# Three passes on high and low halves for the q, k, v projections of a fused attention and feed-forward kernel

## The chip, the core and the metric

The kernel runs on one core of a Trainium2 chip. Time is device time in microseconds (us) of one execution; the median of several runs counts. The core has a matrix engine (TensorE, in the profile PE, its weight loads PEld), a vector engine (VectorE, DVE), an activation engine (ScalarE, ACT), GpSimd (POOL) and a queue for transfers (SyncE, SP). Each engine works off its own list of instructions in order; the lists are tied together by semaphores.

## The reference

`x` has 64 batches of 32 rows by 512 numbers. With C = 32 rows per batch, the computation is, in float32 where nothing else is said:

```python
W = cond_w[condition]                        # one 32x32 matrix per batch
xm = einsum('bct,bcd->bdt', x, W)            # the mix
q, k, v = split(xm @ Wqkv + bqkv)            # 512 -> 3 x 128
a = softmax(q @ k.T / sqrt(128))             # 32 x 32 per batch
x2 = x + (a @ v) @ Wo + bo                   # 128 -> 512
g = sigmoid(conv5(mean of x2 over the first length[b] of 512 columns))
h = dequant(quantize_mx(x2 * g))             # fp8 e4m3, one power of two per 32 numbers
out = x2 + bfloat16(h @ dequant(quantize_mx(ffn_w)).T + ffn_b)
```

## The kernel before

The 2048 rows are 16 tiles of 128 rows (four batches each); two tiles are a unit, so there are 8 units u = 0 to 7, and t = 0 or 1 is the tile in its unit. The quantiser treats the two halves of the weight `ffn_w` as steps 0 and 1 and unit u as step u + 2.

For a unit TensorE does, in this order of dependence: `mix(u, t)` (ps_mix, eight float32 matmuls of 128 columns), `project_qk(u, 0)` for q, `project_qk(u, 1)` for k and `project_v(u)` (four float32 matmuls of 256 columns each, from `wqkv_f` and `xc`), `scores`, `attend` (probabilities times v), `project_out(u, t)` (with Wo), `convolve`, then two loop steps later `ffn(u, t)`. Between them ScalarE copies PSUM to SBUF: `copy_mix` writes `xc` from ps_mix, `copy_qk` q_t and k_t, `copy_v_t`, `copy_v`, `copy_o`, `copy_ffn`; it also makes the exponentials and, as `magnitude`, the absolute values for the rounding. VectorE does the softmax (`score_max` writes negmax; `softmax_inverse`, `softmax_divide`, then four `softmax_turn` write prob_t), the residual sums x2 out of ps_wo, `masked_sum`, `block_max`, the scales (scale, inv, inv_g), `scaled` (h), `round_sum` (h_sum), `round_back` (h_round) and `clip`. GpSimd does `residual` (xb = x + bo), `dequantise` (xq) and most of `final_sum` (result).

The order on each engine is written out by hand. The loop over s = 0 to 6 holds on TensorE: transposes of step s, `turn_v(s)`, `project_qk(s+1, 0)`, `attend(s)`, `mix(s+2, .)`, `project_out(s, 0)`, `project_qk(s+1, 1)`, `project_out(s, 1)`, `scores(s+1)`, `ffn(s-2, 0)`, `project_v(s+1)`, `convolve(s)`, `ffn(s-2, 1)`. `project_out(s, 1)` waits for VectorE's residual sum of tile 0, since both use the bank ps_wo. `convolve(s)` waits for `masked_sum(s, 1)`. GpSimd's `residual(s+1)` stands behind `final_sum(s-2, 1)`, which waits for `copy_ffn(s-2, 1)` on ScalarE and so for `ffn(s-2, 1)`. On ScalarE `copy_mix(s+2, 1)` stands behind `copy_qk(s+1)`, which waits for `project_qk(s+1, 1)`.

Ahead of the loop VectorE works on the weight halves (steps 0 and 1 of the quantiser) and the band matrix of the convolution while the first transfers land, and ScalarE issues four small transfers of `mix_w` itself: `gather_unit_1((2, 3))` stands behind `magnitude(0, 0)` and `magnitude(0, 1)`.

Of the kernel before, what the change touches and what calls it, by code (L numbers as in the profile page):

```python
# [52 lines left out]
def adaln_attn_ffn_kernel(  # L53
# [32 lines left out]
    with ExitStack() as ctx:  # L86
        def sb(name, shape, dt):
            return ctx.enter_context(nc.sbuf_tensor(name, shape, dt))
# [321 lines left out]
        def _(pe):  # L410
# [19 lines left out]
            def project_qk(u, which):  # L430

                if which == 0:
                    if u == 0:
# [8 lines left out]
                if which == 1:  # L442
                    mm.then_inc(qk_done, 1)

            def project_v(u):
# [3 lines left out]
                for c in range(TC):
                    mm = nc.tensor.matmul(ps_v[:], wqkv_f[:, c, 2 * D:3 * D], xc[:, u % 2, c, :],  # L450
                                          start=(c == 0), stop=(c == TC - 1))
                mm.then_inc(v_done, 1)
# [647 lines left out]
```

## Time and profile before

| | |
|---|---|
| time, median of 3 runs | 169.82 us (169.04 to 169.82) |
| time of the profiled execution | 170.97 us |
| its span, first to last instruction | 169.3 us |
| busy: PE, DVE, ACT, POOL | 130.5, 134.9, 65.4, 64.6 us |
| mean granted TensorE clock | 0.879 of full |

The profiled execution lies 1.15 us above the median, and 1.7 us of it are outside its span. "Busy" adds up the time in which an engine had an instruction under way; it doesn't say which engine the end waits for, which is read from the chain of waits and from the order of time.

### The profile page before, as it was taken

How to read it: one execution, taken by the hardware profiler on the slowest of the kernel's cores; microseconds unless marked ns; L12 is line 12 of the kernel's file. 1: busy time of each engine (PE TensorE's matmuls, PEld its weight loads, DVE VectorE, ACT ScalarE, POOL GpSimd, SP SyncE). 2: the span in 40 equal slices, each digit the busy share in tenths (PEclk: the TensorE clock that was granted, in tenths of full speed). 3: DMA queues.
4: the chain of work that ended last, by engine and by line, in shares of the span. 5: the costliest groups of instructions: out<-in, count | busy, mean ns of one | idle time of the engine just before them, and what ended most of it. 6: DMA issues, size and time to landing. Idle time of an engine off the chain costs nothing.

```text
span 169.3 us, 2698 instructions
## 1 busy us (share of the span) xinstructions
PE 130.5 (77%) x738; PEld 90.4 (53%) x738; DVE 134.9 (80%) x279; ACT 65.4 (39%) x158; POOL 64.6 (38%) x48
## 2 busy tenths in 40 slices
PE   6902899699679889959994999499929955947492
PEld 2402789586477676647573867376716633323130
DVE  4198299759987989899989797978799699599932
ACT  0110433554552646426451545144523463106321
POOL 5330058005612902580555055505551553254500
PEclk9985559999978999999999699959995996587959
DMA  4979103040400000042016001100110011101033
GB/s 112 330 216 321 41 15 122 4 129 6 129 8 2 0 0 0 12 148 98 4 64 187 9 3 64 62 0 0 66 62 0 0 62 62 46 18 41 25 124 124
DMA packets 9489, 11.49 MB, mean 68 GB/s; under 512 B 3954, under 2 KB 4466, under 8 KB 9474
## 3 DMA queue, kind: packets, MB, share of 16 engines
q1 hardware_dynamic: 7186, 8.62, 15.2%
q10 hardware_dynamic: 2096, 2.64, 4.9%
q0 software_dynamic: 192, 0.05, 0.5%
q8 instruction: 6, 0.10, 0.2%
q14 instruction: 9, 0.07, 0.2%
HBM read 7.12 MB, written 4.19 MB: 67 GB/s over the span
## 4 chain that ended last, share of the span: by engine, by line
PE 65%; issue 13%; DVE 6%; DMA 5%; POOL 3%; ACT 3%; SPq 2%; POOLq 1%; ACTq 0%; DVEq 0%
PE ps_qk L439 17%; PE ps_mix L426 12%; PE ps_wo L498 10%; PE ps_v L450 8%; PE ps_ffn L535 7%; DMA mix_w<-in_L_cond_weights_dram 5%; PE ps_att L481 3%; POOL xq L373 2%; PE ps_ffn L533 2%; PE ps_att L471 2%; DVE inv_g L929 1%; PE ps_v L460 1%; SPq L303 1%; PE ps_tr L517 1%; DVE mix_w L972 1%
## 5 line engine op out<-in xcount | busy, mean ns | idle before, releaser
L373 POOL TENSOR_TENSOR xq<-h_clip,scale 128x1024 bf16<-128x1024 bf16 (+1 forms) x11 | 23.1, 2104 | 55.8 <-DVE h_clip L967 37.3
L439 PE MATMUL ps_qk<-xc,wqkv_f 128*128 128x256 f32 x128 | 33.1, 407 | 0.8 <-ACT xc L648 0.8
L439 PEld LDWEIGHTS ps_qk<-xc,wqkv_f 128*128 128x128 f32 x128 | 26.3, 210 | 9.2 <-issue 5.9
L426 PE MATMUL ps_mix<-mix_w,x_sb 128*128 128x128 f32 x128 | 20.8, 331 | 7.5 <-DMA mix_w<-in_L_cond_weights_dram 7.5
L426 PEld LDWEIGHTS ps_mix<-mix_w,x_sb 128*128 128x128 f32 x128 | 19.7, 242 | 8.0 <-issue 7.9
L656 ACT ACTIVATE h_mag<-h 128x512 bf16<-128x512 f32 x20 | 12.4, 625 | 27.4 <-DVE h L941 27.4
L294 POOL TENSOR_TENSOR result<-ffn_out,x 128x512 f32<-128x512 bf16 x12 | 14.5, 1208 | 20.7 <-ACT ffn_out L715 20.7
L498 PE MATMUL ps_wo<-wo_f,o_t 128*128 128x512 f32 x30 | 19.0, 722 | 1.0 <-ACT o_t L663 1.0
L363 POOL TENSOR_TENSOR xb<-x_sb,bo_row 128x1024 f32<-128x1024 f32 x8 | 19.2, 2397 | 0.0
L950 DVE SCALAR_TENSOR_TENSOR h_sum<-h_mag,h 128x512 f32<-128x512 bf16 x20 | 13.7, 691 | 6.8 <-ACT h_mag L656 5.9
L481 PE MATMUL ps_att<-prob_t,v_sb 128*128 128x128 f32 x32 | 5.9, 311 | 15.9 <-issue 15.9
L535 PE MATMUL ps_ffn<-wq_t,xq_t 128*128 128x512 bf16 x56 | 17.0, 433 | 0.0
L450 PE MATMUL ps_v<-xc,wqkv_f 128*128 128x256 f32 x64 | 15.3, 383 | 0.0
L855 DVE TENSOR_TENSOR x<-ps_wo,xb 128x512 f32<-128x512 f32 x15 | 10.3, 688 | 5.4 <-PE ps_wo L498 5.3
L481 PEld LDWEIGHTS ps_att<-prob_t,v_sb 128*128 128x128 f32 x32 | 4.7, 207 | 18.4 <-issue 18.3
L648 ACT ACTIVATE xc<-ps_mix 128x512 f32<-128x512 f32 x16 | 9.6, 597 | 11.8 <-PE ps_mix L426 11.8
L958 DVE SCALAR_TENSOR_TENSOR h_round<-h_mag,h_sum 128x1024 bf16<-128x1024 bf16 (+1 forms) x11 | 12.4, 1128 | 1.0
L450 PEld LDWEIGHTS ps_v<-xc,wqkv_f 128*128 128x128 f32 x64 | 12.0, 190 | 2.1
L715 ACT ACTIVATE ffn_out<-ps_ffn 128x512 bf16<-128x512 f32 x14 | 8.3, 596 | 12.3 <-PE ps_ffn L535 12.3
L864 DVE SCALAR_TENSOR_TENSOR masked<-pos_f,len_f,x 128x512 f32<-128x512 f32 x16 | 12.9, 805 | 0.0
L671 ACT ACTIVATE q_t<-ps_qk,bq_scaled 128x256 f32<-128x256 f32 x8 | 3.8, 473 | 21.1 <-PE ps_qk L439 21.1
L941 DVE TENSOR_TENSOR h<-x,inv_g 128x512 f32<-128x512 f32 x16 | 11.3, 749 | 0.2
(86 smaller groups left out, 198.0 us busy)
## 6 DMA issues: line engine op xcount, KB each, us to landing
out_dram<-result SPq DMA_DIRECT2D x16, 256.0 KB, 2.0
x_sb<-in_x_dram SPq DMA_DIRECT2D x7, 512.0 KB
ffn_w_f<-in_L_ffn_weight_dram ACTq DMA_DIRECT2D x2, 512.0 KB, 8.6
mix_w<-in_L_cond_weights_dram SPq DMA_DIRECT2D x56, 4.0 KB, 1.6
wqkv_f<-in_L_attn_Wqkv_dram ACTq DMA_DIRECT2D x1, 768.0 KB, 5.4
x_sb<-in_x_dram SPq DMA_DIRECT2D x2, 256.0 KB, 6.4
bias_row<-in_L_ffn_bias_dram ACTq DMA_DIRECT2D x1, 256.0 KB, 5.6
bo_row<-in_L_attn_bo_dram ACTq DMA_DIRECT2D x1, 256.0 KB, 7.6
```

Source lines behind the costliest of these rows:

```text
L294: engine.tensor_tensor(result[:, t, :], ffn_out[:, t, :], x2[:, u % 3, t, :], ALU.add) \
L363: nc.gpsimd.tensor_tensor(xb[:, u % 2], x_sb[:, u], bo_row[:].to_broadcast([P, SUB, T]), ALU.add) \
L373: nc.gpsimd.tensor_tensor(xq[:, v % 2, t0:t1].rearrange("p t (n k) -> p (t n) k", k=BLOCK), h_clip[:, v % 2, t0:t1].rearrange("p t (n k) - ...
L426: mm = nc.tensor.matmul(ps_mix[t][:, c, :], x_sb[:, u, t, c * P:(c + 1) * P], mix_w[:, u, t, :], start=True, stop=True)
L439: mm = nc.tensor.matmul(ps_qk[:, which, :], wqkv_f[:, c, which * D:(which + 1) * D], xc[:, u % 2, c, :], start=(c == 0), stop=(c == TC - 1))
L450: mm = nc.tensor.matmul(ps_v[:], wqkv_f[:, c, 2 * D:3 * D], xc[:, u % 2, c, :], start=(c == 0), stop=(c == TC - 1))
L481: mm = nc.tensor.matmul(ps_o[:, t * P:(t + 1) * P], v_sb[:, u % 2, t, :], prob_t[:, t, :], start=True, stop=True)
L498: nc.tensor.matmul(wo_bank(u, t), o_t[:, tok], wo_f[:], start=True, stop=True) \
L535: mm = nc.tensor.matmul(bank, xq_t[:, u % 2, c, t * P:(t + 1) * P], wq_t[:, c, :], start=False, stop=(c == TC - 1))
L656: nc.scalar.activation(h_mag[:, v % 2, t, :], h[:, v % 2, t, :], ACT.Abs, scale=ROUND_GAIN).then_inc(h_mag_done, 1)
L864: nc.vector.scalar_tensor_tensor(out=masked[:, t, :], in0=pos_f[:], scalar=len_f[:, i:i + 1], in1=x2[:, u % 3, t, :], op0=ALU.is_lt, op1=A ...
L950: nc.vector.scalar_tensor_tensor(out=h_sum[:, t, :], in0=h_mag[:, v % 2, t, :], scalar=ROUND_FLOOR, in1=h[:, v % 2, t, :], op0=ALU.max, op ...
```

## The change

Each of the two operands of the q, k, v projections is kept as two tiles of the type float32r, high and low: `hi` is the value as ScalarE rounds it to that type, `lo` the difference to the float32 value. The product is formed as hi·hi + lo(weight)·hi + hi·lo(x), accumulated in the same PSUM bank, so each projection has 12 matmuls of 256 columns where it had 4. ScalarE's `copy_mix` writes `xc_hi` where it wrote `xc`; VectorE's new `split_mix_lo(u, t)` reads ps_mix again and writes `xc_lo`. The weight is split once: `round_wqkv` on ScalarE, `split_wqkv_lo` on VectorE. The product with Wo, the mix, the scores and the attention stay float32.

```diff
-                for c in range(TC):
-                    mm = nc.tensor.matmul(ps_qk[:, which, :],
-                                          wqkv_f[:, c, which * D:(which + 1) * D],
-                                          xc[:, u % 2, c, :], start=(c == 0), stop=(c == TC - 1))
+                steps = passes(u)
+                for n in range(first * TC, last * TC):
+                    w, xt, c = steps[n]
+                    if n == 2 * TC and which == 0:
+                        pe.wait_ge(xc_lo_done, SUB * (u + 1))
+                    mm = nc.tensor.matmul(ps_qk[:, which, :], w[:, c, which * D:(which + 1) * D],
+                                          xt[:, c, :], start=(n == 0), stop=(n == len(steps) - 1))
...
             mix(0, 0)
             mix(0, 1)
-            project_qk(0, 0)
+            project_qk(0, 0, 0, 2)
+            project_v(0, 0, 2)
+            project_qk(0, 0, 2, 3)
+            project_v(0, 2, 3)
             project_qk(0, 1)
-            project_v(0)
...
+            def round_wqkv():
+                act.wait_ge(wqkv_loaded, 16)
+                nc.scalar.activation(wqkv_hi[:], wqkv_f[:], ACT.Copy).then_inc(wqkv_hi_done, 1)
...
             late_loads()
+            round_wqkv()
             copy_mix(0, 0)
...
+            def split_wqkv_lo():
+                dve.wait_ge(wqkv_hi_done, 1)
+                nc.vector.tensor_tensor(wqkv_lo[:], wqkv_f[:], wqkv_hi[:].bitcast(F32),
+                                        ALU.subtract).then_inc(wqkv_lo_done, 1)
+
+            def split_mix_lo(u, t):
+
+                if u >= 2:
+                    dve.wait_ge(v_done, u - 1)
+                dve.wait_ge(xc_hi_done, SUB * u + t + 1)
+                tok = slice(t * P, (t + 1) * P)
+                nc.vector.tensor_tensor(xc_lo[:, u % 2, :, tok], ps_mix[t][:],
+                                        xc_hi[:, u % 2, :, tok].bitcast(F32), ALU.subtract) \
+                    .then_inc(xc_lo_done, 1)
...
             iotas()
+            split_wqkv_lo()
+            split_mix_lo(0, 0)
+            split_mix_lo(0, 1)
             block_max(0, 0)
...
             scale_inverse(1)
+            split_mix_lo(1, 0)
             score_max(0)
+            split_mix_lo(1, 1)
             scaled(1, 0)
...
                 round_back(s + 1)
+                if is_unit(s + 2):
+                    split_mix_lo(s + 2, 0)
                 residual_sum(s, 0)
                 clip(s + 1)
+                if is_unit(s + 2):
+                    split_mix_lo(s + 2, 1)
                 masked_sum(s, 0)
```

On TensorE, in a step of the loop, the row between two products with Wo (ps_wo) is the k projection. Before:

```order
L426 MATMUL ps_mix<-mix_w,x_sb 128x128 x8
L498 MATMUL ps_wo<-wo_f,o_t 128x512
L439 MATMUL ps_qk<-xc,wqkv_f 128x256 x4
L498 MATMUL ps_wo<-wo_f,o_t 128x512
L471 MATMUL ps_att<-k_t,q_t 32x32 x8
```

and in the changed kernel:

```order
L432 MATMUL ps_mix<-mix_w,x_sb 128x128 x8
L519 MATMUL ps_wo<-wo_f,o_t 128x512
L456 MATMUL ps_qk<-xc_hi,wqkv_hi 128x256 x4
L456 MATMUL ps_qk<-xc_hi,wqkv_lo 128x256 x4
L456 MATMUL ps_qk<-xc_lo,wqkv_hi 128x256 x4
L519 MATMUL ps_wo<-wo_f,o_t 128x512
L492 MATMUL ps_att<-k_t,q_t 32x32 x8
```

Four matmuls have become twelve in the same place; q and v change likewise.

On VectorE ahead of the loop (amax to h are step 0 of the quantiser, the rows with same and band_k are the band matrix). Before:

```order
L783 TENSOR_SCALAR ident_f<-diag_f 128x128
L878 TENSOR_REDUCE amax<-ffn_w_f 128x16 x2
L909 TENSOR_SCALAR amax_e<-amax 128x32
L916 TENSOR_SCALAR scale<-amax_e 128x32
L923 TENSOR_SCALAR inv<-scale 128x32
L941 TENSOR_TENSOR h<-ffn_w_f,inv 128x512 x2
L801 MEMSET same 128x128
```

and in the changed kernel:

```order
L811 TENSOR_SCALAR ident_f<-diag_f 128x128
L851 TENSOR_TENSOR wqkv_lo<-wqkv_f,wqkv_hi 128x1536
L860 TENSOR_TENSOR xc_lo<-ps_mix0,xc_hi 128x4x128
L860 TENSOR_TENSOR xc_lo<-ps_mix1,xc_hi 128x4x128
L921 TENSOR_REDUCE amax<-ffn_w_f 128x16 x2
L952 TENSOR_SCALAR amax_e<-amax 128x32
L959 TENSOR_SCALAR scale<-amax_e 128x32
```

The work on the weight half now stands behind three instructions, two of which need unit 0's mix.

On VectorE in the loop, from the rounding of step s + 1 to the masked sum of unit s. In the changed kernel:

```order
L1001 SCALAR_TENSOR_TENSOR h_round<-h_mag,h_sum 128x1024
L860 TENSOR_TENSOR xc_lo<-ps_mix0,xc_hi 128x4x128
L898 TENSOR_TENSOR x2<-ps_wo,xb 128x512
L1010 TENSOR_SCALAR h_clip<-h_round 128x1024
L860 TENSOR_TENSOR xc_lo<-ps_mix1,xc_hi 128x4x128
L907 SCALAR_TENSOR_TENSOR masked,ysum<-pos_f,len_f,x2 128x512
```

The two rows at L860 are new; the other four stood next to each other in this order.

## Rows read from the trace of the kernel before

**Rows 1.** The page: busy time, share of the span, instructions.
```profile
PE 130.5 (77%) x738; PEld 90.4 (53%) x738; DVE 134.9 (80%) x279; ACT 65.4 (39%) x158; POOL 64.6 (38%) x48
```

**Rows 2.** Chain that ended last: start, us, what; the loop step s = 3.
```profile
77.23 1.79 PE ps_mix L426 x16
...
79.88 1.73 PE ps_qk L439 x8
...
83.23 0.86 PE ps_ffn L535 x4
84.10 1.73 PE ps_v L450 x8
...
89.44 2.40 issue
...
92.53 2.91 PE ps_mix L426 x16
```

**Rows 3.** Timeline of the same step: start, us, engine, line, instruction.
```profile
80.65 0.69 DVE L855 TENSOR_TENSOR x<-ps_wo,xb 128x512 f32<-128x512 f32 x1
...
82.37 0.60 ACT L648 ACTIVATE xc<-ps_mix 128x512 f32<-128x512 f32 x1
...
83.59 1.07 DVE L864 SCALAR_TENSOR_TENSOR masked<-pos_f,len_f,x 128x512 f32<-128x512 f32 x1
...
85.30 0.17 DVE L831 RECIPROCAL prob_inv<-psum_row 128x2 f32<-128x2 f32 x1
...
85.66 0.28 PE L505 MATMUL ps_wo<-ysum,band 128*128 128x2 f32 x2
...
87.08 0.60 ACT L715 ACTIVATE ffn_out<-ps_ffn 128x512 bf16<-128x512 f32 x1 [0.32 <-PE ps_ffn L535]
...
87.75 1.16 POOL L294 TENSOR_TENSOR result<-ffn_out,x 128x512 f32<-128x512 bf16 x1 [1.78 <-ACT ffn_out L715]
...
88.87 2.34 POOL L363 TENSOR_TENSOR xb<-x_sb,bo_row 128x1024 f32<-128x1024 f32 x1
...
89.25 2.00 DVE L923 TENSOR_SCALAR inv<-scale 128x32 int32<-128x32 int32 x1
...
91.50 0.24 DVE L847 STREAM_TRANSPOSE prob_t<-prob_n 32x64 f32<-32x64 f32 x1
```

**Rows 4.** Groups by line and shape: busy, mean ns of one, idle before.
```profile
L855 DVE TENSOR_TENSOR x<-ps_wo,xb 128x512 f32<-128x512 f32 x15 | 10.3, 688 | 5.4 <-PE ps_wo L498 5.3 <-issue 0.2
...
L648 ACT ACTIVATE xc<-ps_mix 128x512 f32<-128x512 f32 x16 | 9.6, 597 | 11.8 <-PE ps_mix L426 11.8
```

**Rows 5.** Timeline ahead of the loop and into its first step.
```profile
11.14 1.27 DVE L878 TENSOR_REDUCE amax<-ffn_w_f 128x16 f32<-128x512 f32 x2
...
17.55 0.29 DVE L818 TENSOR_TENSOR band<-band_k,same 128x128 f32<-128x128 f32 x1
...
19.76 0.60 ACT L648 ACTIVATE xc<-ps_mix 128x512 f32<-128x512 f32 x1 [1.11 <-PE ps_mix L426]
...
20.91 1.29 DVE L950 SCALAR_TENSOR_TENSOR h_sum<-h_mag,h 128x512 f32<-128x512 bf16 x2 [3.06 <-ACT h_mag L656]
...
23.64 1.19 DVE L967 TENSOR_SCALAR h_clip<-h_round 128x1024 bf16<-128x1024 bf16 x1
...
30.10 0.23 DVE L825 TENSOR_REDUCE negmax<-ps_att 128x2 f32<-128x64 f32 x1 [0.67 <-PE ps_att L471]
...
31.89 1.04 DVE L847 STREAM_TRANSPOSE prob_t<-prob_n 32x64 f32<-32x64 f32 x4
...
33.98 0.61 PE L481 MATMUL ps_att<-prob_t,v_sb 128*128 128x128 f32 x4
```

**Rows 6.** Stretches: us, busy PE PEld DVE ACT POOL, PEclk, DMA, GB/s.
```profile
76.55:91.84 15.29, 12.83 (x86) 9.34 (x87) 13.95 (x29) 7.03 (x18) 6.92 (x4) 1.00 0.22 66
91.84:108.57 16.73, 14.43 (x86) 10.81 (x87) 13.85 (x29) 7.04 (x18) 6.92 (x4) 0.90 0.16 55
...
92.53:96.82 4.29, 4.29 (x19) 3.54 (x19) 3.15 (x4) 2.82 (x5) 0.00 (x0) 0.60 0.09 24
```

More of the change, by code:

```diff
@@ L97, in adaln_attn_ffn_kernel @@
         wqkv_f = sb("wqkv_f", [P, TC, 3 * D], F32)
+        wqkv_hi = sb("wqkv_hi", [P, TC, 3 * D], F32R)
+        wqkv_lo = sb("wqkv_lo", [P, TC, 3 * D], F32R)
         wo_f = sb("wo_f", [P, T], F32)
@@ L126, in adaln_attn_ffn_kernel @@
         mix_w = sb("mix_w", [P, UNITS, SUB, P], F32)
-        xc = sb("xc", [P, 2, TC, TOK], F32)
+        xc_hi = sb("xc_hi", [P, 2, TC, TOK], F32R)
+        xc_lo = sb("xc_lo", [P, 2, TC, TOK], F32R)
         q_t = sb("q_t", [P, 2, TOK], F32)
@@ L213, in adaln_attn_ffn_kernel @@
         mix_done = sem("mix_done")
-        xc_done = sem("xc_done")
+        wqkv_hi_done = sem("wqkv_hi_done")
+        wqkv_lo_done = sem("wqkv_lo_done")
+        xc_hi_done = sem("xc_hi_done")
+        xc_lo_done = sem("xc_lo_done")
         exp_done = sem("exp_done")
@@ L428, in mix, with passes, project_qk @@
                 mm.then_inc(mix_done, 1)
-            def project_qk(u, which):
-                if which == 0:
+            def passes(u):
+                hi, lo = xc_hi[:, u % 2], xc_lo[:, u % 2]
+                return [(a, b, c) for a, b in ((wqkv_hi, hi), (wqkv_lo, hi), (wqkv_hi, lo))
+                        for c in range(TC)]
+            def project_qk(u, which, first=0, last=3):
+                if which == 0 and first == 0:
                     if u == 0:
-                        pe.wait_ge(wqkv_loaded, 16)
+                        pe.wait_ge(wqkv_hi_done, 1)
+                        pe.wait_ge(wqkv_lo_done, 1)
@@ L435, in project_qk @@
                     else:
                         pe.wait_ge(k_copied, u)
-                    pe.wait_ge(xc_done, SUB * (u + 1))
-                for c in range(TC):
-                    mm = nc.tensor.matmul(ps_qk[:, which, :],
-                                          wqkv_f[:, c, which * D:(which + 1) * D],
-                                          xc[:, u % 2, c, :], start=(c == 0), stop=(c == TC - 1))
-                if which == 1:
+                    pe.wait_ge(xc_hi_done, SUB * (u + 1))
@@ L443, in project_qk, with project_v @@
+                steps = passes(u)
[5 more added lines that the diff above has]
+                                          xt[:, c, :], start=(n == 0), stop=(n == len(steps) - 1))
+                if which == 1 and last == 3:
                     mm.then_inc(qk_done, 1)
-            def project_v(u):
-                if u >= 1:
+            def project_v(u, first=0, last=3):
+                if u >= 1 and first == 0:
@@ L448, in project_v @@
                     pe.wait_ge(v_copied, u)
[L449 to L452, printed above, removed]
+                steps = passes(u)
+                for n in range(first * TC, last * TC):
+                    w, xt, c = steps[n]
+                    if n == 2 * TC:
+                        pe.wait_ge(xc_lo_done, SUB * (u + 1))
+                    mm = nc.tensor.matmul(ps_v[:], w[:, c, 2 * D:3 * D], xt[:, c, :],
+                                          start=(n == 0), stop=(n == len(steps) - 1))
@@ L454, in turn_v @@
+                if last == 3:
+                    mm.then_inc(v_done, 1)
             def turn_v(u):
@@ L647, in copy_mix @@
                 tok = slice(t * P, (t + 1) * P)
-                nc.scalar.activation(xc[:, u % 2, :, tok], ps_mix[t][:], ACT.Copy) \
-                    .then_inc(xc_done, 1)
+                nc.scalar.activation(xc_hi[:, u % 2, :, tok], ps_mix[t][:], ACT.Copy) \
+                    .then_inc(xc_hi_done, 1)
             def magnitude(v, t):
```

4 lines of the change are left out of this document (2 added, 2 removed).

## The prediction

> **What bounds the kernel now.** The page comes first: TensorE is busy for 130.5 us and VectorE for 134.9 us [rows 1], so neither alone fills the span, and the order of time decides. The chain of waits then shows one loop step, attend(3) at 76.55 to attend(4) at 91.84 [rows 2, 6]. TensorE goes through mix (1.79), Wo, the k projection (1.73), scores, ffn, the v projection (1.73), ffn without a gap; behind the q projection it stands for 2.40 us before attend [rows 2]. The timeline says why: VectorE's last prob_t starts at 91.50, behind an inv that took 2.00 us, from 89.25, just as long as GpSimd's xb (88.87 to 91.21) was still running [rows 3]. That inv has 32 numbers in a row; it is held, not working. And xb starts there because result precedes it (87.75), which waited for ffn_out (87.08), which waited for the second ffn of TensorE [rows 3]. So the cycle of a step is TensorE's work from attend to the second ffn, then ScalarE 0.60, GpSimd 1.16 + 2.34, then VectorE's last pieces. The q projection lies beside the GpSimd part and is free already.
>
> The second limit is close behind. In the same step VectorE is busy for 13.95 of 15.29 us, TensorE for 12.83 [rows 6]. About 2 us of VectorE's are the hold, and its masked sum of tile 1 (83.59 + 1.07) ends 1 us ahead of the convolution at 85.66 [rows 3]. What is put in front of the masked sum has 1 us of cover and no more.
>
> **TensorE's part of the change.** Four float32 matmuls of 256 columns take 1.73 us, 0.43 each; four bf16 matmuls of 512 columns take 0.86 [rows 2], so 0.108 for 256 columns. The mix, eight float32 matmuls of 128 columns in 16 passes, takes 1.79, or 0.112 a pass with a float32 weight load each. No row shows a float32r matmul. Its bounds are 0.108 (as bf16 by column) and 0.43 (as float32 now). I take 0.112: 12 matmuls are then 1.34 us against 1.73, a saving of 0.39 per projection. On the cycle lie k and v, so 0.78 us per step; q's 0.39 only lengthens the stand before attend. Were a matmul 0.216, twice the low bound, a projection would take 2.59 and cost 0.86 more; at 0.43 it would cost 3.46 more.
>
> The Trainium skill, "FP8 and Floating Point Precision", section TensorE Precision Notes, says that full float32 is four passes (high and low by high and low) and that reduced float32 is read in 4 bytes and truncated. By it the new projection is three passes against four, 1.30 us, which is nearly the sum's value; the 1.73 for four matmuls agrees with four passes at the bf16 rate.
>
> **VectorE's part in the loop.** A split of a tile reads 128x512 float32 of PSUM and as much of SBUF and writes float32, in shape the residual sum, 0.688 us [rows 4]. Two per step are 1.38 us, ahead of masked_sum, in the steps s = 0 to 5 (s = 6 has none). The first stands behind h_round, and its high half has been copied by then: no wait. The second stands behind clip and needs copy_mix(s+2, 1), which ran 82.37 to 82.97 [rows 3]; with k 0.39 shorter it ends at 82.6. VectorE would come to it behind h_round, the first split (80.65 + 0.69), the residual sum (0.69) and the clip, which I put at 0.3 to 0.4: at 82.35, so it waits 0.2 to 0.3. Masked_sum(s, 1) then ends at 84.66 + 1.38 + 0.25 = 86.3, or 86.0 where it isn't the 1.07 us form; the convolution, on TensorE 85.66 before and 84.9 by its own work now, comes at 86.0 to 86.3: 0.3 to 0.6 late instead of 0.78 early. The second ffn, ffn_out, result and xb follow it. The softmax pieces, 1.6 later than before, fall under the same hold of xb, which has only moved by 0.3 to 0.6. So with the full clock a step is 15.6 to 15.9, near 15.7: TensorE's 0.78 is spent on VectorE's delay and 0.4 more is lost.
>
> In s = 0 there is no ffn to cover anything and VectorE is on the cycle: the two splits and at most 0.5 of waiting for the second copy make that step 1.4 to 1.9 longer.
>
> **The clock.** TensorE stood 2.40 us before attend(4), and the granted clock of the stretch right behind was 0.60 of full [rows 6]: mix took 2.91 instead of 1.79 [rows 2], and that step 16.73 us instead of 15.29 [rows 6]. Now TensorE works 1.17 us less in a step and stands longer: about 2.8 before attend (2.40 + 0.39) and some 0.9 before the convolution. I expect the lower level, 1.2 GHz, after most attends. Then mix and the first Wo take up to 1.8 + 0.4 more, the k projection ends, and copy_mix(s+2, 1) with it, 2.2 later; VectorE waits for that copy at the second split, and everything behind it (masked 0 and 1, two block maxima, residual 1, negmax: 3.8 us) follows. Masked_sum(s, 1) ends near 11.8 us behind attend instead of 8.1, and a step comes to about 17.5. Of the six steps with splits I take two at 15.7 and four at 17.5.
>
> **Ahead of the loop.** VectorE's work from 11.14 to 17.84 (the first weight half and the band matrix, 6.70 us) was free: it lay beside the wait for the first mix, and VectorE stood 3.06 us at h_sum (20.91) even so [rows 5]. Now it stands behind the two splits of unit 0. The second high half is copied 19.76 to 20.36 [rows 5], its split ends at 21.1, the 6.70 us end at 27.8, and h_sum starts there instead of at 20.91: 6.9 late. The clip that took 1.19 (23.64) was held and need not be: back 0.8, so 6.1. The split of tile 0 of unit 1 takes the 0.67 us for which negmax waited at 30.10 [rows 5]: negmax at 36.2. The next split needs a high half that ScalarE copies behind two exponentials, which wait for that negmax: copied at about 37.6, split at 38.3, where h stood at 30.2. So prob_t, whose last piece ended at 32.93, ends at 41.1. TensorE was not waiting for it; it began attend(0) at 33.98 [rows 5]. Now it waits: 41.1, or 7.1 us late. The float32 split of the weight (128x1536, an estimate of three times 0.69) fits between 11.14 and the first copy, and `round_wqkv` (three times 0.597) before 18: both free. ScalarE stands at magnitude for h until about 25, so its last two mix_w transfers are late, mix(1, 1) runs near 29, and scores(0) by 31; they stay ahead of negmax at 36.2.
>
> **Sum.** Start 7.1. Step 0: +1.9, and +1.6 if at the low level: 3.3 taken. Step 1: between nothing and step 0's 1.9, +1.3. Steps 2 to 5: before, two at the full clock, counted as 15.2, and two like the 16.73 of [rows 6], 63.9; now one at 15.7 and three at 17.5, 68.2: +4.3. Step 6, without splits, keeps part of TensorE's 0.78: -0.3. Together 15.7. The profiled time, 170.97, becomes 186.7; against the median, 1.15 lower, 185.5. The clock term is the softest of them; if it comes in half as often as I take it, 3.5 us go, so I put the time at 184.
>
> **Rivals.**
> 1. The clock holds or is no worse than before (a case of the forecast's mechanism, but priced apart): start 7.1, step 0 +1.9, steps 2 to 5 at 15.7 -1.1, the rest -0.6: 7.3, or 177 us. For it: the whole step from 76.55 ran at 1.00 [rows 6], so not every stand brings a drop. Against it: every stand gets longer. Chance 0.17.
> 2. A float32r matmul of 256 columns costs 0.216 or more. For it: a weight load of 128x128 float32 has its own row beside every matmul, and if load and stream didn't overlap they would add to this. Then k and v cost 0.86 each where they saved 0.39, 1.25 more twice in seven steps, 17 us less what VectorE's own delay covers (some 7): 194 us; TensorE would stand less and keep the clock. Against it: mix runs at 0.112 a pass with a load in each. Chance 0.13.
> The Trainium skill, "TensorE: Matmul & The Clock Gate", section Weight-path perf modes, says that the fast weight load isn't given to float32 input; that a load takes about the columns at 1.2 GHz (section LDWEIGHTS) would put it at 107 ns, just under a matmul of 256 columns at full clock. If hidden it changes nothing, if not it is this rival.
> 3. Not slower: TensorE's cycle rules, and VectorE's new work lies under the hold and the start in slack. It decides if VectorE has over 2.4 us of real slack ahead of masked_sum in each step, instead of 1, and if prob_t of unit 0 isn't what attend(0) waits for. Then seven steps save 0.78, 5.5 us: 164.5. Against it: the hand-written order on VectorE, in which nothing can pass the 6.70 us behind the mix. Chance 0.06.
> 4. The float32r type brings nothing, 0.43 a matmul: 3.46 more for k and v in seven steps, about 45: 225. Chance 0.02.
> 5. The start costs less (its work is overtaken by a wait elsewhere) and steps cancel: within 0.5% of before, chance 0.03.
>
> The forecast has 0.59. The range takes in rival 1 and reaches into rival 2: 175 to 193. A difference under 0.5% is what a measurement of this kernel can't tell from none. Slower 0.91, same 0.03, faster 0.06.
>
> **What the profile of the changed kernel would show.** Right: ps_qk matmuls of about 110 ns pitch; VectorE waiting for xc_hi at 13 to 20 us and amax starting at 21; attend(0) at 41; two xc_lo rows of 0.69 per step; TensorE waiting for masked at the convolution; masked_sum(s, 1) later against attend by 1.5 us or more; more low clock digits. Wrong: attend(0) before 38, a ps_qk pitch of 0.2 or more, steps as long as before with VectorE's stands grown shorter, or a convolution that never waits.

## The result, and the profile after

The changed kernel takes 184.06 us (median of 4 runs, 182.49 to 188.00) against 169.43 for the kernel before beside it (4 runs, 168.68 to 169.82): a ratio of 1.084, interval 1.074 to 1.094. The forecast was 184.0 and slower. The profiled execution took 184.79 us with a span of 183.1, 13.8 longer than the span of before. Times with a range below are medians of all executions, while the ratios and their intervals leave out those that are over 1.5% above the fastest of their kernel, so what a change is worth is taken from the ratios where the two differ. Where an execution profiled below lies off its kernel's median by over 1%, its own time stands beside it.

The page, as [rows 1]. TensorE is busy for 2.9 us less with 96 more rows (a float32 matmul has two rows in the trace, a float32r one has one), VectorE for 10.0 us more; the groups below it show 11.0 us of splits and that VectorE stood 16.2 us for the high half.

```profile
PE 127.6 (70%) x834; PEld 95.1 (52%) x834; DVE 144.9 (79%) x296; ACT 67.7 (37%) x159; POOL 62.0 (34%) x48
...
L860 DVE TENSOR_TENSOR xc_lo<-ps_mix,xc_hi 128x512 fp32r<-128x512 f32 x16 | 11.0, 688 | 16.2 <-ACT xc_hi L675 16.2
```

The timeline ahead of the loop, as [rows 5].

```profile
9.15 1.48 ACT L640 ACTIVATE wqkv_hi<-wqkv_f 128x1536 fp32r<-128x1536 f32 x1
...
10.66 1.76 DVE L851 TENSOR_TENSOR wqkv_lo<-wqkv_f,wqkv_hi 128x1536 fp32r<-128x1536 f32 x1
...
18.81 0.69 DVE L860 TENSOR_TENSOR xc_lo<-ps_mix,xc_hi 128x512 fp32r<-128x512 f32 x1 [6.39 <-ACT xc_hi L675]
...
21.12 1.27 DVE L921 TENSOR_REDUCE amax<-ffn_w_f 128x16 f32<-128x512 f32 x2
...
28.61 1.28 DVE L993 SCALAR_TENSOR_TENSOR h_sum<-h_mag,h 128x512 f32<-128x512 bf16 x2
...
36.85 0.21 DVE L868 TENSOR_REDUCE negmax<-ps_att 128x2 f32<-128x64 f32 x1
...
40.53 1.04 DVE L890 STREAM_TRANSPOSE prob_t<-prob_n 32x64 f32<-32x64 f32 x4
...
41.72 0.63 PE L502 MATMUL ps_att<-prob_t,v_sb 128*128 128x128 f32 x4
```

VectorE stands for 6.39 us at a split, with the weight half and the band matrix queued behind it; amax starts 10.0 later than in [rows 5], h_sum 7.7, and attend(0) 7.7.

The chain of waits through the step from attend(3) to attend(4), as [rows 2].

```profile
89.36 3.25 PE ps_mix L432 x16
...
93.65 1.42 PE ps_qk L456 x12
95.46 0.47 ACT k_t L700
95.93 0.50 ACT xc_hi L675
97.12 0.75 DVE masked L907 x2
...
99.21 0.78 DVE masked L907 x2
100.03 0.38 PE ps_wo L526 x2
...
102.19 1.40 PE ps_qk L456 x12
103.59 2.53 issue
```

In [rows 2] the chain never left TensorE between mix and the stand before the next attend. Now it leaves it behind the k projection, goes over the copy of the high half to VectorE's masked sums, and comes back at the convolution. The timeline of the same step, as [rows 3]:

```profile
92.79 0.68 DVE L860 TENSOR_TENSOR xc_lo<-ps_mix,xc_hi 128x512 fp32r<-128x512 f32 x1
...
94.94 1.91 POOL L379 TENSOR_TENSOR xq<-h_clip,scale 128x1024 bf16<-128x1024 bf16 x1 [6.68 <-DVE x L898]
...
96.52 0.69 DVE L860 TENSOR_TENSOR xc_lo<-ps_mix,xc_hi 128x512 fp32r<-128x512 f32 x1 [1.71 <-ACT xc_hi L675]
97.12 0.74 DVE L907 SCALAR_TENSOR_TENSOR masked<-pos_f,len_f,x 128x512 f32<-128x512 f32 x1
...
100.03 0.38 PE L526 MATMUL ps_wo<-ysum,band 128*128 128x2 f32 x2 [1.09 <-DVE masked L907]
...
103.36 2.34 POOL L369 TENSOR_TENSOR xb<-x_sb,bo_row 128x1024 f32<-128x1024 f32 x1
103.47 2.27 DVE L972 TENSOR_TENSOR inv_g<-inv,gate 128x32 f32<-128x32 f32 x1
```

The convolution waits for masked (1.09 us); in this step of the kernel before it waited for nothing. The hold by xb is still there: inv_g, 32 numbers in a row, takes 2.27.

Three stretches, as [rows 6]: attend(2) to (3), attend(3) to (4), and attend(7) to the end; then the last one of before.

```profile
72.69:88.68 15.99, 12.18 (x100) 9.23 (x99) 14.09 (x30) 7.17 (x18) 6.55 (x4) 1.00 0.16 48
88.68:106.12 17.44, 13.71 (x99) 10.86 (x99) 14.74 (x31) 7.15 (x18) 6.55 (x4) 0.90 0.21 65
...
156.99:183.10 26.11, 15.67 (x64) 7.23 (x64) 19.19 (x33) 8.68 (x16) 8.31 (x5) 0.84 0.16 61
```

```profile
141.55:169.30 27.75, 18.34 (x64) 8.12 (x64) 19.19 (x33) 8.67 (x16) 8.03 (x5) 0.77 0.16 58
```

The starts of attend(0) to attend(7), read from the timelines, give the whole balance (us):

| | attend(0) | step 0 | 1 | 2 | 3 | 4 | 5 | 6 | rest | span |
|---|---|---|---|---|---|---|---|---|---|---|
| before | 33.98 | 13.83 | 13.66 | 15.08 | 15.29 | 16.73 | 16.75 | 16.23 | 27.75 | 169.3 |
| after | 41.72 | 15.78 | 15.19 | 15.99 | 17.44 | 17.43 | 17.43 | 16.01 | 26.11 | 183.1 |
| difference | +7.74 | +1.95 | +1.53 | +0.91 | +2.15 | +0.70 | +0.68 | -0.22 | -1.64 | +13.8 |

The start costs 7.7 us, the seven steps cost 7.7 more, and the rest gives back 1.6. Steps 0 and 1 of the changed kernel have a stretch at the low clock that isn't behind attend but behind TensorE's stand ahead of the convolution (2.02 and 2.70 us), over the transposes and the q projection: their granted clock is 0.89 each, where the kernel before had 1.00 and 0.88 (its step 1 had the low clock behind attend(1)). In step 1:

```profile
68.64 0.38 PE L526 MATMUL ps_wo<-ysum,band 128*128 128x2 f32 x2 [2.70 <-DVE masked L907]
...
71.53 0.24 DVE L890 STREAM_TRANSPOSE prob_t<-prob_n 32x64 f32<-32x64 f32 x1
...
72.69 0.60 PE L502 MATMUL ps_att<-prob_t,v_sb 128*128 128x128 f32 x4
```

The last prob_t is there at 71.77 and attend(2) starts at 72.69, behind the slow q projection, so the low clock costs up to 0.9 us in this step. In step 0 TensorE stood 1.70 us before attend(1) even so, and it costs nothing.

### The profile page after: what moved, and what is told of

Read it like the earlier page. It is cut to its first block, busy times and chain, and to the rows that moved or that the text cites. A ratio compares the mean times of both kernels' runs of the same rounds, so it can differ in the third digit from the quotient of the medians.

```text
span 183.1 us, 2920 instructions
## 1 busy us (share of the span) xinstructions
PE 127.6 (70%) x834; PEld 95.1 (52%) x834; DVE 144.9 (79%) x296; ACT 67.7 (37%) x159; POOL 62.0 (34%) x48
## 4 chain that ended last, share of the span: by engine, by line
PE 43%; DVE 27%; issue 14%; DMA 7%; ACT 5%; SPq 2%; DVEq 0%; ACTq 0%
PE ps_qk L456 13%; PE ps_mix L432 10%; DVE masked L907 7%; PE ps_wo L519 5%; DMA mix_w<-in_L_cond_weights_dram 4%; DVE amax L921 4%; PE ps_ffn L556 4%; PE ps_att L502 3%; ACT xc_hi L675 2%; PE ps_tr L538 2%; DMA out_dram<-result 2%; DVE x L898 2%; DVE h L984 2%; PE ps_v L481 2%; DVE result L300 2%
## 5 line engine op out<-in xcount | busy, mean ns | idle before, releaser
L379 POOL TENSOR_TENSOR xq<-h_clip,scale 128x1024 bf16<-128x1024 bf16 (+1 forms) x11 | 20.8, 1895 | 61.3 <-DVE h_clip L1010 32.2
L432 PEld LDWEIGHTS ps_mix<-mix_w,x_sb 128*128 128x128 f32 x128 | 20.9, 254 | 9.5 <-issue 9.5
L860 DVE TENSOR_TENSOR xc_lo<-ps_mix,xc_hi 128x512 fp32r<-128x512 f32 x16 | 11.0, 688 | 16.2 <-ACT xc_hi L675 16.2
L683 ACT ACTIVATE h_mag<-h 128x512 bf16<-128x512 f32 x20 | 12.5, 626 | 29.4 <-DVE h L984 29.4
L519 PE MATMUL ps_wo<-wo_f,o_t 128*128 128x512 f32 x30 | 17.9, 682 | 1.6 <-DVE x L898 1.1
L502 PE MATMUL ps_att<-prob_t,v_sb 128*128 128x128 f32 x32 | 6.5, 336 | 15.7 <-issue 15.7
L456 PE MATMUL ps_qk<-xc_hi,wqkv_hi 128*128 128x256 f32 x64 | 16.4, 387 | 0.8 <-ACT xc_hi L675 0.8
L907 DVE SCALAR_TENSOR_TENSOR masked<-pos_f,len_f,x 128x512 f32<-128x512 f32 x16 | 14.3, 896 | 0.0
L456 PEld LDWEIGHTS ps_qk<-xc_hi,wqkv_hi 128*128 128x128 f32 x64 | 11.3, 234 | 5.0 <-issue 5.0
L502 PEld LDWEIGHTS ps_att<-prob_t,v_sb 128*128 128x128 f32 x32 | 5.1, 225 | 16.7 <-issue 16.7
L675 ACT ACTIVATE xc_hi<-ps_mix 128x512 fp32r<-128x512 f32 x16 | 9.6, 598 | 8.7 <-PE ps_mix L432 8.7
L456 PE MATMUL ps_qk<-xc_hi,wqkv_lo 128*128 128x256 f32 x64 | 12.2, 322 | 0.0
L972 DVE TENSOR_TENSOR inv_g<-inv,gate 128x32 f32<-128x32 f32 x8 | 11.9, 1493 | 0.3
L984 DVE TENSOR_TENSOR h<-x,inv_g 128x512 f32<-128x512 f32 x16 | 11.3, 749 | 0.2
```

Source lines behind the costliest of these rows:

```text
L379: nc.gpsimd.tensor_tensor(xq[:, v % 2, t0:t1].rearrange("p t (n k) -> p (t n) k", k=BLOCK), h_clip[:, v % 2, t0:t1].rearrange("p t (n k) - ...
L456: mm = nc.tensor.matmul(ps_qk[:, which, :], w[:, c, which * D:(which + 1) * D], xt[:, c, :], start=(n == 0), stop=(n == len(steps) - 1))
L502: mm = nc.tensor.matmul(ps_o[:, t * P:(t + 1) * P], v_sb[:, u % 2, t, :], prob_t[:, t, :], start=True, stop=True)
L519: nc.tensor.matmul(wo_bank(u, t), o_t[:, tok], wo_f[:], start=True, stop=True) \
L907: nc.vector.scalar_tensor_tensor(out=masked[:, t, :], in0=pos_f[:], scalar=len_f[:, i:i + 1], in1=x2[:, u % 3, t, :], op0=ALU.is_lt, op1=A ...
L984: nc.vector.tensor_tensor(h[:, v % 2, t, :].rearrange("p (n k) -> p n k", k=BLOCK), src[:, t, :].rearrange("p (n k) -> p n k", k=BLOCK), b ...
```

## Experiments

**1. The start.** The splits of unit 0 moved behind the band matrix, nothing else.

```
             split_wqkv_lo()
-            split_mix_lo(0, 0)
-            split_mix_lo(0, 1)
             block_max(0, 0)
...
             band_matrix()
+            split_mix_lo(0, 0)
+            split_mix_lo(0, 1)
             round_sum(0, 0)
```

> The changed kernel with one thing moved: VectorE's two splits of unit 0 stand behind the first weight half and the band matrix instead of ahead of them. Theory (the start is late because 6.7 us of VectorE's work stand behind splits that wait for the mix): amax starts near 12.5 instead of 21.1, h_sum near 21 instead of 28.6, attend(0) comes near 36 instead of 41.9 (the splits of unit 1 stay where they are), and the time is 5 to 6 us under the changed kernel's, 178 to 179 us. Rival (the start is late because ScalarE issues two transfers of mix_w late, or because of the split of the weight): attend(0) stays within 1 us of 41.9, 183 to 184 us.

178.25 us (176.54 to 178.88), ratio 1.048 (1.039 to 1.058). Its timeline:

```profile
18.95 0.68 DVE L860 TENSOR_TENSOR xc_lo<-ps_mix,xc_hi 128x512 fp32r<-128x512 f32 x1
20.35 0.69 DVE L860 TENSOR_TENSOR xc_lo<-ps_mix,xc_hi 128x512 fp32r<-128x512 f32 x1 [0.72 <-ACT xc_hi L675]
20.96 1.28 DVE L993 SCALAR_TENSOR_TENSOR h_sum<-h_mag,h 128x512 f32<-128x512 bf16 x2
...
34.82 1.01 PE L502 MATMUL ps_att<-prob_t,v_sb 128*128 128x128 f32 x4
```

h_sum is back at 20.96 (20.91 in [rows 5]) and attend(0) comes 6.9 us earlier than in the changed kernel. The loop's steps change by 0.4 at most (16.16, 15.36, 16.00, 17.44, ...). So 6.9 of the 7.7 are the place of two instructions in an engine's queue, not their 1.4 us of work.

**2 and 3. One engine's part alone.** First VectorE's: the copies and splits are made, but the projections read float32 in four matmuls (the low halves are read by nothing, and `xc_hi` is a float32 tile here, so the splits of x do the same work and give zeros).

```
-                return [(a, b, c) for a, b in ((wqkv_hi, hi), (wqkv_lo, hi), (wqkv_hi, lo))
-                        for c in range(TC)]
+                return [(wqkv_f, hi, c) for c in range(TC)]
```

> VectorE's and ScalarE's part of the change alone: all splits and both weight halves are made as in the changed kernel, but q, k and v are formed by the four float32 matmuls of before from the float32 weight and the copied mix; the low halves are not read by TensorE. Theory (the loss is VectorE's new work at its places): attend(0) near 42, steps 3 to 5 as long as in the changed kernel or up to 0.6 longer, in all 184 to 188 us. Rival (the loop's loss is TensorE's lower clock, which comes from its having less to do): the loop runs as before, only the start's 7.7 us are lost, 176 to 178 us.

Then TensorE's: twelve float32r matmuls, the splits of x left out. The third pass adds the product of the high halves again, so the product with the low half of x isn't computed.

```
-                ... ((wqkv_hi, hi), (wqkv_lo, hi), (wqkv_hi, lo))
+                ... ((wqkv_hi, hi), (wqkv_lo, hi), (wqkv_hi, hi))
...
-                if is_unit(s + 2):
-                    split_mix_lo(s + 2, 0)
...
-                if is_unit(s + 2):
-                    split_mix_lo(s + 2, 1)
```

> TensorE's part alone: twelve float32r matmuls per projection, weight halves made, but no split of the mix; the third pass reads the high half of x again, so the low half of x is left out of the result. Theory: attend(0) near 34, k and v 0.3 us shorter each on the cycle of a step, seven steps, 164.5 to 166.5 us. Rival (shorter projections let the clock fall more often, which eats the gain): 168 to 172 us, with steps of 16.7 us or more where before had 15.1 to 15.3.

| splits | projections | us | ratio (interval) |
|---|---|---|---|
| no | float32 (before) | 169.96 | 1 |
| no | float32r (3) | 167.08 | 0.980 (0.970 to 0.990) |
| yes | float32 (2) | 187.96 | 1.097 (1.087 to 1.108) |
| yes | float32r (after) | 184.06 | 1.084 (1.074 to 1.094) |

By the ratios, TensorE's part alone gives 3.4 us, and with the splits there some 2.3, though those two intervals overlap; 14 matmul groups (k and v in seven steps) shortened by 0.31 would give 4.3. VectorE's part alone costs 16.5. A theory in which the halves of the change share the loss falls: the loss is VectorE's. 3 lies between what its two theories gave. Its low clock came behind attend(1), (3) and (4) (a granted clock of 0.66 over the 5 us behind each), three times as in the kernel before, so it isn't the clock that kept it from the first theory's 166.5. Its step 2, at the full clock, took 14.63 us instead of 15.08: on its own the shorter k and v do shorten a step, by about 0.5 us and not by the 0.78 of the forecast.

**4. The clock.** Eight bf16 matmuls with zeros, into a PSUM bank whose contents are already copied out, before every attend that has a mix behind it, to see what the low clock costs.

```
+            def fill(u, n=8):
+                pe.wait_ge(xc_lo_done, SUB * (u - 1) + 1)
+                bank = ps_mix[0][:].rearrange("p c k -> p (c k)")
+                for _ in range(n):
+                    nc.tensor.matmul(bank, warm[:, 0:P], warm[:], start=True, stop=True)
...
                 project_qk(s + 1, 0)
+                if is_unit(s + 2):
+                    fill(s + 2)
                 attend(s)
```

> The changed kernel with eight bf16 matmuls of 512 columns on zeros (into ps_mix's bank, which is free there) between the q projection and attend in the steps that have a mix, 1.7 us of work in a stand of 2.5 us. Theory (the lower clock behind the stand lengthens the step through mix, Wo, k, the second copy and the split): mix of units 5 to 7 takes 1.8 instead of 2.9 to 3.3 us, steps 3 to 5 come to 15.7 to 16 us instead of 17.4, the time to 178 to 180 us. Rival (the step's length is set by VectorE's load and the hold of GpSimd's xb, not by the clock): mix is shorter but the steps stay at 17.2 to 17.5, 183 to 184 us.

187.59 us (185.84 to 189.39), ratio 1.102 (1.090 to 1.115). Every mix ran at the full clock, and the kernel is not faster: attend(0) came at 44.01 instead of 41.72 and step 1 took 17.04 instead of 15.19, since TensorE had no stand to fill before attend(0) and attend(2); before attend(1), where it had 1.70 us, step 0 grew by 0.34 only. Steps 3 to 5 took 16.61 instead of 17.44. Both expectations missed, for two reasons: the fill's cost where nothing stood, and a smaller value of the clock than I had put. The second shows in the timeline of step 3, attend(3) at 93.18:

```profile
99.04 1.91 POOL L379 TENSOR_TENSOR xq<-h_clip,scale 128x1024 bf16<-128x1024 bf16 x1 [6.28 <-DVE x L907]
...
99.39 0.69 DVE L869 TENSOR_TENSOR xc_lo<-ps_mix,xc_hi 128x512 fp32r<-128x512 f32 x1 [0.48 <-ACT xc_hi L684]
...
100.00 1.50 DVE L916 SCALAR_TENSOR_TENSOR masked<-pos_f,len_f,x 128x512 f32<-128x512 f32 x1
```

With the copy earlier, the masked sum comes while GpSimd's xq still runs and takes 1.50 instead of 0.74: it ends 0.55 us behind the end of xq at 100.95. The split, which lies in xq's time too, takes its 0.69.

**5. The splits behind the masked sums.** Experiment 1, and both splits of the loop moved behind block_max(s + 2, 1).

```
                 masked_sum(s, 1)
                 block_max(s + WBLOCKS, 1)
+                if is_unit(s + 2):
+                    split_mix_lo(s + 2, 0)
+                    split_mix_lo(s + 2, 1)
```

> The kernel of e1_start with the two splits of a loop step moved behind block_max(s+2, 1), so that nothing of them stands ahead of masked_sum(s, 1). The amount of work on VectorE is the same. Theory (the place costs, not the amount: ahead of the masked sum a split delays convolution, ffn, result and xb, behind it it lies under the stand that xb causes anyway): TensorE no longer waits at the convolution, steps 3 to 5 come to 15.0 to 16.4 us, 170 to 173 us. Rival (VectorE is full, 1.4 us more per step must show wherever they stand): 176 to 179 us, no less than e1_start by more than 1.

175.80 us (174.94 to 176.11), ratio 1.039 (1.028 to 1.050): 2.45 under experiment 1, between the two expectations; the intervals of the two overlap. The other steps took 13.66 to 16.30, but step 3 took 19.70. Its timeline:

```profile
87.25 1.91 POOL L379 TENSOR_TENSOR xq<-h_clip,scale 128x1024 bf16<-128x1024 bf16 x1 [8.47 <-DVE h_clip L1010]
87.26 2.46 DVE L907 SCALAR_TENSOR_TENSOR masked<-pos_f,len_f,x 128x512 f32<-128x512 f32 x1
...
95.68 2.34 POOL L369 TENSOR_TENSOR xb<-x_sb,bo_row 128x1024 f32<-128x1024 f32 x1
95.85 2.20 DVE L952 TENSOR_SCALAR amax_e<-amax_g 128x32 uint32<-128x32 uint32 x1
```

Without the split ahead of it, masked starts 0.01 us behind xq and is held for all of it; later amax_e is held by xb, with the softmax pieces behind it. Which of two instructions starts first decides here 1.7 us of masked (2.46 for 0.74). The step is 3.6 longer than the next (16.11); its low clock also lasted longer (a granted clock of 0.85 against 0.91 over the step), and this run doesn't part the two. From this the next question: are the holds, not the work, what the three passes collide with?

**6 and 7. The softmax pieces ahead of the scale chain,** so that xb can't hold them; first in the kernel before, then in the changed one with the moves of 1 and 5.

```
+                for j in range(JB):
+                    softmax_turn(s, j)
                 if s + 1 >= WBLOCKS:
                     gate_denominator(s + 1)
...
-                softmax_turn(s, 0)
...
-                softmax_turn(s, 3)
```

> The kernel before with one thing moved on VectorE: the four pieces of prob_t come directly behind prob_n, ahead of the chain of the scales (gate, amax_e, scale, inv, inv_g), in the steps of the loop. Theory (attend waits for the hold of inv or inv_g by GpSimd's xb, because prob_t's last piece is queued behind it): attend starts right behind the q projection, the stand of 2.2 to 2.8 us before it is gone, the clock stays up, a step is 13.8 to 14.8 us, and the time is 160 to 165 us. Rival (VectorE's h chain takes over as the limit, since VectorE is busy for 14 of 15.3 us): the stand only moves to another place (transposes or Wo), 168 to 170 us.

> Both moves in the changed kernel: splits of unit 0 behind the band matrix, splits of a step behind block_max(s+2, 1), pieces of prob_t first. Now prob_t stands behind the splits with no hold to cover them. Theory: VectorE becomes the limit with 1.4 us more than in e6_turns_first, TensorE stands for it, 4 to 9 us over e6_turns_first. Rival (TensorE's shorter projections show once its stand is gone): within 2 us of e6_turns_first or under it.

6: 166.45 us (165.39 to 167.27), ratio 0.984 (0.973 to 0.996), between its two expectations. The step from 88.44 to 103.57 took 15.13, and TensorE's stand has moved from attend to the first product with Wo, which waits for a copy on ScalarE that stands behind the late h_mag:

```profile
88.03 2.35 POOL L363 TENSOR_TENSOR xb<-x_sb,bo_row 128x1024 f32<-128x1024 f32 x1
88.15 2.27 DVE L916 TENSOR_SCALAR scale<-amax_e 128x32 f32<-128x32 f32 x1
...
92.64 1.13 PE L498 MATMUL ps_wo<-wo_f,o_t 128*128 128x512 f32 x2 [1.81 <-ACT o_t L663]
```

7: 171.14 (170.48 to 172.02), ratio 1.015 (1.004 to 1.025), 4.7 over 6 (5.2 by the ratios), in the range of its theory. The mechanism is only in part the one expected. The spans of the two profiled executions differ by 3.8 us, and 3.2 of it lie in two steps, step 3 with 17.30 for 15.12 and step 4 with 16.10 for 15.13, while step 5 took 15.05 for 15.14 with the splits in it. In both of the long ones TensorE stood 2.58 instead of 1.81 ahead of the first product with Wo, and the clock behind it was the low one (0.66 over the 5 us from 79.0), where 6 kept the full one; in step 3 masked was also held for 2.46 again. What each of these costs isn't shown.

**8 and 9. xb earlier.** GpSimd's residual(s + 1), which makes xb, directly behind dequantise(s + 1); alone (8), and with the order of 6 (9).

```
+            residual(0)
             for s in range(UNITS - 1):
-                residual(s)
                 dequantise(s + 1)
+                residual(s + 1)
...
-            residual(UNITS - 1)
             final_sum(nc.gpsimd, UNITS - 3, 0)
```

> The kernel before with GpSimd's xb of unit s+1 directly behind dequantise(s+1), ahead of the two results. Theory (the step is set by the chain ffn, result, xb, hold, prob_t): xb ends 2 us or more earlier and holds prob_n instead of inv, the last result holds scale until about 1.5 us before attend came; steps are 1 to 2 us shorter, 160 to 166 us. Rival (only the time at which VectorE is held changes, not the sum): 168 to 171 us.

> The kernel before with both reorderings: the pieces of prob_t first on VectorE, xb of unit s+1 directly behind dequantise(s+1) on GpSimd. Theory (each of the two takes the hold away from the piece that attend waits for; together there is nothing more to take): 159 to 162 us, steps of 14.0 to 14.4. Rival (the two add up, as TensorE then has no stand at all): 156 to 158 us.

8: 161.53 (160.89 to 162.39), ratio 0.955 (0.945 to 0.965), with the float32 projections of before. One instruction moved on GpSimd gives 4.5%, 7.7 us. Steps 2 and 3 fell from 15.08 and 15.29 to 14.39. Steps 4 and 5 fell from 16.73 and 16.75 to 14.38, since the low clock that the kernel before had there didn't come; an estimated 3 us of the gain is this (16.7 less 15.3, twice). 9: 158.88 (157.33 to 160.63; 160.63 is the profiled one), ratio 0.937 (0.931 to 0.942), the fastest of all, and 0.1 under the range of its theory. In 8, xb runs beside other rows and what it holds is cheaper:

```profile
99.67 2.80 POOL L363 TENSOR_TENSOR xb<-x_sb,bo_row 128x1024 f32<-128x1024 f32 x1
...
101.11 1.45 DVE L835 TENSOR_TENSOR prob_n<-prob,prob_inv 128x64 f32<-128x64 f32 x1
```

**10 and 11. The three passes in that better order.** 10: the changed kernel with the moves of 1, 5 and 8. 11: with those of 1 and 8, the loop's splits left where the change put them.

> e5_splits_late with xb directly behind dequantise(s+1) as in e8_xb_early: the three passes with the splits behind the masked sum and without the late hold. Theory (VectorE's 1.4 us per step now lie bare, since xb no longer holds prob_t, while TensorE saves 0.6): steps of 14.8 to 15.2 us against 14.38 in e8_xb_early, 165 to 168 us, so slower than e8_xb_early. Rival (TensorE is the limit once the hold is gone, so that the three passes pay): 158 to 161 us.

> e1_start with xb early: the loop's splits stay where the change put them, ahead of the masked sum. Theory (the waits of VectorE for the second copy stay, and masked_sum stays late): steps of 15.3 to 16 us, 168 to 171 us, 2 to 4 us over e10_late_xb. Rival (the place no longer matters when the hold has moved): within 1 us of e10_late_xb.

10: 162.70 (161.82 to 164.00), ratio 0.958 (0.950 to 0.966). 11: 171.66 (11 runs, 167.86 to 175.63), ratio 0.997 (0.991 to 1.002). The step from 92 us on, of 8, then of 10:

```profile
92.16:106.54 14.38, 12.83 (x87) 9.34 (x87) 13.66 (x29) 7.04 (x18) 7.30 (x4) 1.00 0.23 76
```

```profile
92.27:106.68 14.41, 12.00 (x99) 9.26 (x99) 13.73 (x31) 7.05 (x18) 7.33 (x4) 1.00 0.22 76
```

TensorE works 0.83 us less in the step of 10 and the step is as long: its stand before attend is 2.31 us instead of 1.49. So in the best place that I found for the splits the three passes gain nothing in the loop and lose little: 10 and 8 have ratios of 0.958 and 0.955 and aren't told apart. 10 came out 2.3 us under its theory's range, which had VectorE's 1.4 us lie bare. They don't, and VectorE's busy time shows it, 13.73 against 13.66 with two splits more. In 10 both splits run while xb does, and are not held:

```profile
99.78 2.82 POOL L369 TENSOR_TENSOR xb<-x_sb,bo_row 128x1024 f32<-128x1024 f32 x1
...
100.90 1.27 DVE L860 TENSOR_TENSOR xc_lo<-ps_mix,xc_hi 128x512 fp32r<-128x512 f32 x2
...
102.28 0.41 DVE L878 TENSOR_TENSOR prob_n<-prob,prob_inv 128x64 f32<-128x64 f32 x1
```

They fill the time for which prob_n was held in 8 (1.45, here 0.41). One step of 10 is longer, step 3 with 15.76 between 14.43 and 14.41, all three at a granted clock of 1.00. There masked and xq start together again, as in step 3 of experiment 5:

```profile
81.77 1.91 POOL L379 TENSOR_TENSOR xq<-h_clip,scale 128x1024 bf16<-128x1024 bf16 x1 [7.08 <-DVE h_clip L1010]
...
81.77 2.46 DVE L907 SCALAR_TENSOR_TENSOR masked<-pos_f,len_f,x 128x512 f32<-128x512 f32 x1
```

With the clock out of it, that step is 1.3 us longer than its neighbours: so much the step loses by it where xq starts first. The splits' place is worth 6.5 us between 10 and 11 by their ratios, more than the 2 to 4 expected; that part of my theory was too small. The runs of 11 spread by 4.5%, so I read no single step of it.

**12. The fill where TensorE stood.** Experiment 4 with the fill ahead of attend(3), (4) and (5) alone.

```
-                if is_unit(s + 2):
+                if 3 <= s and is_unit(s + 2):
                     fill(s + 2)
```

> The changed kernel with the eight filling matmuls of e4_fill only ahead of attend(3), attend(4) and attend(5), where TensorE stood for 2.5 us and the mix behind ran at the lower clock. Theory (what the lower clock costs a step is 0.8 us, as between 17.44 in the changed kernel and 16.61 in e4_fill, and the rest of e4_fill's loss came from filling where there was no stand): mix 1.8 us, steps 3 to 5 at 16.6 us, the time 2 to 3 us under the changed kernel's 184.06, at 181 to 182.5 us. Rival (the filling itself costs, wherever it stands): 184 us or more.

182.46 (6 runs, 180.35 to 185.69; 180.35 is the profiled one), ratio 1.073 (1.064 to 1.082). By time alone it isn't told from the changed kernel, since the intervals overlap; the windows do it. Its step from attend(3):

```profile
88.17:104.77 16.60, 14.03 (x107) 10.03 (x107) 15.43 (x31) 7.15 (x18) 6.56 (x4) 1.00 0.20 63
```

16.60 at a granted clock of 1.00 against 17.44 at 0.90: three such steps are worth 2.5 us, all that the low clock behind attend cost in the steps with splits. The rival of this run, that filling costs wherever it stands, is out by these windows.

## Why the prediction was right, and where it wasn't

**The start** was foreseen by its mechanism and within 0.8 us: h_sum at 28.6 for 27.8, negmax at 36.85 for 36.2, attend(0) at 41.7 for 41.1. The weight's split was free (1.48 and 1.76 us, both done before 12.5). Experiment 1 shows it by undoing it.

**The second split and the masked sum.** The split cost the 0.688 us of [rows 4] to the nanosecond. The convolution came late in every split step, as forecast; the wait for the high half was 1.71 us at the low clock, and masked_sum(s, 1) ended 11.3 us behind attend(3), for 11.8. Forecast for a step were 15.7 us at the full clock and 17.5 at the low one; measured were 15.99 and 17.44. The sum for steps 2 to 5, one at the full clock and three at the low, gave +4.3 and was +4.4.

**The float32r matmul** was taken at 0.112 us and was 0.118 (twelve in 1.40 to 1.42), so a projection saved 0.31 and not 0.39. The prediction's reason for its value was not sound: it read the 16 rows of the mix as passes of 0.112, but they are two rows for each of eight matmuls of 128 columns, and by the same count the k projection's eight rows of 256 columns are 0.216 each. That a matmul came out near 0.112 is luck in that argument; its lower bound, 0.108 by bf16, was the sound one. Rival 2, a matmul of 0.216, and rival 4 are out. By the Trainium skill, "FP8 and Floating Point Precision", section TensorE Precision Notes, which gives true float32 four passes, three passes in place of four would be an estimated 1.30; the trace has 1.40 to 1.42, a little more than passes alone. Why isn't shown by any run here.

**Terms that were mis-sized.** Step 0 was put at +3.3, because I counted the price of a low clock there; it was +1.95, as much as the two splits and the wait (1.4 to 1.9 were forecast for that part). A low clock did come in that step, behind the stand ahead of the convolution, but in front of another stand, where it cost nothing. The low clock came behind attend(3), (4) and (5), three of the six split steps and not four. The kernel before had it three times as well, behind attend(1), (4) and (5) (0.66 over the 5 us behind each); I had read it off steps 2 to 5 alone. So behind attend the change moved the low clock and did not add to it; the stretches in steps 0 and 1 came on top, and one of them cost up to 0.9 us. The rest of the loss is VectorE's queue, as experiments 2 and 3 have it. Rival 1 had all of steps 2 to 5 at 15.7; three were at the low clock, and experiment 12 shows that they would have been 16.60 without it, so its 177 would not have come with the full clock either. The tail was put at 0 and gave back 1.64: VectorE's busy time there is the same 19.19, but the granted clock was 0.84 instead of 0.77 and TensorE's busy time 15.67 instead of 18.34. The sum for the span was 15.7 against 13.8, and the 1.5 us that I had taken off (185.5 to 184) for doubt about the clock brought the forecast to the measured time. That agreement is in part luck: step 0 and the tail, not the clock in steps 2 to 5, are what the doubt stood for.

**The clock's price** was wrong in its step. I had priced it as the difference of two steps, 17.5 less 15.7. Experiments 4 and 12 give 0.83 us. The step that failed is the one that has everything behind the second copy move with it: at the full clock the masked sum moves into xq's time instead and waits there (1.50 us for 0.74).

**What the prediction did not see** is that masked itself can be held. It read the hold of VectorE by xb in [rows 3] and used it for the small pieces at the end of a step; the 1.07 us form of masked in the same rows, with xq of GpSimd then on its way, was the same thing:

```profile
81.81 2.30 POOL L373 TENSOR_TENSOR xq<-h_clip,scale 128x1024 bf16<-128x1024 bf16 x1 [5.68 <-DVE x L855]
```

xq ends at 84.11, and masked ends 0.55 behind it, as in experiments 4 and 5 (0.55 and 0.56). The changed kernel has such holds too: both masked sums of its step 1 took 1.5. The rule stands in the Trainium skill, "SBUF — State Buffer", section Who interferes with whom: a VectorE instruction with two SBUF inputs, or in a mode that uses two ports, and a GpSimd instruction that reads SBUF exclude each other for the whole instruction, whichever starts first; one with at most one SBUF input and no such mode isn't held. The traces agree on all rows shown: masked (two SBUF inputs) 0.74 free, 1.50 and 2.46 held; amax_e and inv_g held 2.20 and 2.27; the split (one input in PSUM) 0.69 each time. For amax_e, with one input, the rule asks for a mode with two ports, which the trace doesn't show. With the rule the danger of experiment 5's order could have been seen; that the two instructions would start 0.01 us apart could not.

**What stays open.** What decides after which stand the clock falls isn't settled: in the kernel before, TensorE stood 2.19 us ahead of attend(3) and of attend(5) alike, and the full clock followed the one and the low clock the other. The spread of experiment 11 has no cause that I tested.

## What to carry to other kernels

An engine works its queue in order, so a new instruction costs what stands behind it while it waits, not its own duration: two splits of 0.69 us put attend(0) 7.7 us late at one place and 0.8 at another. Before shortening TensorE, see whether TensorE's work is on the path: here shorter projections alone gave 2.0% in the order of before (experiment 3), and in the best order 0.83 us less work per step only made TensorE's stand longer. Look for VectorE rows far longer than their size allows, with a GpSimd row ending where they end; moving that one GpSimd instruction gave 4.5% (interval 3.5 to 5.5), more than the shorter arithmetic did. Where new VectorE work can't be held (here the splits), a place beside the GpSimd instruction that would hold its neighbours cost next to nothing in experiment 10.

## What the runs showed of the hardware

- A float32r matmul of 128x128 by 256 columns has a pitch of 0.118 us, where float32 has 0.43 and bf16 0.108 (half of the 0.215 for 512 columns) by [rows 2]; each has its weight load beside it. Copying PSUM to a float32r tile on ScalarE takes 0.60 us for 128x512, as to float32.
- The exclusion works both ways: with masked first (97.31) GpSimd's xq takes 2.30 us in experiment 10; with nothing of VectorE's in its way it takes 1.91.

```profile
97.31 0.74 DVE L907 SCALAR_TENSOR_TENSOR masked<-pos_f,len_f,x 128x512 f32<-128x512 f32 x1
97.52 2.30 POOL L379 TENSOR_TENSOR xq<-h_clip,scale 128x1024 bf16<-128x1024 bf16 x1 [7.08 <-DVE h_clip L1010]
```

- A full clock can be bought with zero matmuls (granted 1.00 over the 5 us behind every filled attend), but it is worth only what the next limit leaves: 0.83 us of a step of 17.44, and less than nothing where TensorE did not stand.
